# First sample by image halves in the opening, last sample stored in blocks, and constant matmuls in pauses of TensorE

## What is computed

```
x = x + _L0_conv_ref(_gn(x), ...)   # 3x3 conv, per-sample mixture of 3 experts, reflect pad
x = x + _L1_conv_ref(_gn(x), ...)   # |x|, depthwise 3x3
x = x + _L2_conv_ref(_gn(x), 8)     # 17x17 box mean
x = x + _L3_conv_ref(_gn(x), ...)   # sum of 8 neighbours, then 5 pointwise layers, 4 of them with elu

def _gn(v, G=8, eps=1e-05):         # mean and variance over 2 channels x 128 x 128
    g = v.reshape(B_, G, C_ // G, H_, W_)
    m = jnp.mean(g, axis=(2, 3, 4), keepdims=True)
    s = jnp.var(g, axis=(2, 3, 4), keepdims=True)
    return ((g - m) / jnp.sqrt(s + eps)).reshape(v.shape)
```

## Time and profile before

| | us |
|---|---|
| time, median of 3 runs (lowest, highest) | 721.12 (719.9, 723.21) |
| the profiled execution's own time | 722.67 |
| its span, first to last instruction | 720.9 |
| PE busy | 606.0 (84%) |
| DVE busy | 579.5 (80%) |
| ACT busy | 555.3 (77%) |
| POOL busy | 321.8 (45%) |

### The profile page before, as it was taken

One profiled execution on the slowest core, in us unless ns is written; L12 is line 12 of the kernel. 1 busy time (PEld: TensorE's weight loads), 2 busy tenths in 40 slices (PEclk: granted clock), 3 DMA queues, 4 the chain that ended last, 5 costly groups with the idle time before them and its releaser, 6 DMA issues.

```text
span 720.9 us, 13382 instructions
## 1 busy us (share of the span) xinstructions
PE 606.0 (84%) x4142; PEld 167.4 (23%) x4142; DVE 579.5 (80%) x1006; ACT 555.3 (77%) x1057; POOL 321.8 (45%) x487
## 2 busy tenths in 40 slices
PE   0355572899999999999999999999999899889981
PEld 0221220222222222222222222222222222222220
DVE  1453655688998899889988998898889788799992
ACT  0232100689999999999999999999999998988882
POOL 2530446136961797078717871777007800810000
PEclk9986676899999999999999999999999999999997
DMA  6769389629377728692868185718521820182002
GB/s 134 152 144 194 68 148 194 127 51 187 89 168 177 156 70 179 147 188 54 188 153 192 37 196 121 168 36 195 126 61 26 203 65 0 43 197 53 1 1 58
DMA packets 72890, 85.53 MB, mean 119 GB/s; under 512 B 8698, under 2 KB 58378, under 8 KB 72842
## 3 DMA queue, kind: packets, MB, share of 16 engines
q1 hardware_dynamic: 65488, 77.06, 49.4%
q10 hardware_dynamic: 7354, 7.87, 5.7%
HBM read 9.14 MB, written 8.39 MB: 24 GB/s over the span
## 4 chain that ended last, share of the span: by engine, by line
PE 45%; DVE 26%; ACT 12%; issue 8%; DMA 4%; SPq 1%; ACTq 1%; DVEq 1%; POOL 1%; POOLq 0%
PE pz L796 20%; PE pc L739 10%; DVE g L1001 8%; PE pc L773 7%; ACT u L659 5%; DVE bn L944 4%; ACT u L662 4%; DVE u L998 3%; DVE g_last L1001 3%; ACT u L665 3%; PE po L739 3%; PE po L805 2%; DMA win<-y 2%; DMA xs<-in_x_dram 2%; DVE xs L985 2%
## 5 line engine op out<-in xcount | busy, mean ns | idle before, releaser
L659 ACT ACTIVATE u<-pz 128x512 f32<-128x512 f32 x472 | 260.6, 601 | 67.4 <-PE pz L796 65.1
L796 PE MATMUL pz<-g,wT 64*64 64x512 f32 x1536 | 272.5, 610 | 18.6 <-DVE g L1001 16.7
L1001 DVE SCALAR_TENSOR_TENSOR g<-u,pz 128x512 f32<-128x512 f32 x384 | 247.9, 681 | 42.0 <-ACT u L662 37.7
L662 ACT ACTIVATE u<-u 128x512 f32<-128x512 f32 x472 | 275.7, 639 | 1.3
L796 PEld LDWEIGHTS pz<-g,wT 64*64 64x64 f32 x1536 | 69.2, 131 | 197.6 <-issue 196.1
L773 PE MATMUL pc<-win,t 64*32 64x512 f32 x1344 | 93.7, 630 | 8.2 <-DMA win<-y 5.8
L796 PE MATMUL pz<-stack,wT 64*64 64x512 f32 x512 | 86.7, 619 | 16.2 <-issue 10.3
L1001 DVE SCALAR_TENSOR_TENSOR g_last<-u,pz 128x512 f32<-128x512 f32 x128 | 82.7, 682 | 21.1 <-ACT u L662 19.3
L944 DVE BATCH_NORM_STATS2 bn<-xs 128x6 f32<-128x512 f32 (+1 forms) x128 | 84.6, 686 | 16.4 <-DMA xs<-in_x_dram 13.8
L739 PE MATMUL pc<-box_sum,box_mat 128*128 128x512 f32 x138 | 74.5, 634 | 1.3 <-DVE box_sum L1017 0.8
L459 POOL TENSOR_TENSOR stat<-stat 128x1 f32<-128x1 f32 x32 | 6.2, 195 | 132.8 <-DVE stat L959 132.8
(11 more groups left out here) (96 smaller groups left out, 504.2 us busy)
## 6 DMA issues: line engine op xcount, KB each, us to landing
stack<-near_sum SPq DMA_DIRECT2D x93, 192.0 KB, 3.9
win<-y SPq DMA_DIRECT2D x54, 260.0 KB, 4.4
win<-y SPq DMA_DIRECT2D x54, 195.0 KB, 4.5
out_dram<-xs SPq DMA_DIRECT2D x8, 1024.0 KB
stack<-box_sum SPq DMA_DIRECT2D x62, 128.0 KB, 3.8
xs<-in_x_dram SPq DMA_DIRECT2D x5, 1024.0 KB
stack<-near_sum SPq DMA_DIRECT2D x31, 128.0 KB, 2.9
win<-y ACTq DMA_DIRECT2D x10, 260.0 KB, 7.1
```

The costliest lines, as they stand in the source:

```text
L659: act.activation(u[:, m, :], pz[:, m, :], ACT.Relu, scale=-1.0, bias=0.0).then_inc(relu_done, 1)
L662: act.activation(u[:, m, :], u[:, m, :], ACT.Exp, scale=-1.0).then_inc(exp_done, 1)
L796: last = pe.matmul(pz[to, m, :], wT[rows, l, rows], src, start=True, stop=True)
L1001: dve.scalar_tensor_tensor(out=elus(l)[:, m, :], in0=u[:, m, :], scalar=-1.0, in1=pz[:, m, :], op0=ALU.add, op1=ALU.max).then_inc(g_writte ...
```

## The change

1. **Windows and convolutions of sample 0 (layers 0 and 1).** The windows are copied per quarter c: SP has c = 0 and 2, ACT c = 1 and 3. There are 26 DMAs for layer 0 (14 before) and 24 for layer 1 (12 before), for the same bytes. Each image half has a semaphore of its own, and `conv_taps` n writes chunks 2n and 2n + 1 and waits for the windows of its half alone. The other samples keep their windows.
2. **Constant matmuls.** `idle_turns(n)` issues n matmuls of 384 columns of the early constants into `po`, which nobody reads at that time. There are 4 behind a new wait for `setup_dve` >= 6, 3 ahead of layer 1 of sample 0, 4 and 5 ahead of and behind two `group_sums`, and 8 ahead of `rounds`: 24 in all.
3. **Last sample.** The store is 16 DMAs of 64 KB, one for each k, on SP except for the last two, which are on ACT. Each follows the `output` of its chunk.
4. **Clipping.** `clipped` no longer holds in the slot behind an `output`: slots 2, 11, 21 and 27 of the last sample and slot 27 of the one before, 5 halves in all, go back to two relus on ACT.

```diff
+        def clipped(j, q, l, a):
+            return (isinstance(j, int) and (j == B - 1 or j == B - 2 and q == Q - 1)
+                    and HALVES * q + 2 * l + a - 1 not in OUTPUT_AT)
...
+        def pair(i, k, n):
+            return (2 * n, 2 * n + 1) if isinstance(i, int) and i == 0 and k < 2 else (n, n + 2)
...
+        def windows_first(eng, k, c, last):
+            y, win, landed = ((y0, win0, win0_first), (y1, win1, win1_first))[k]
+            rows = around(y, win, c * KB, (c + 1) * KB, c % 2, last)
+            if k == 0 and not last and c % 3 == 0:
+                rows.append(edge0(c // 3))
+            for dst, src in rows:
+                eng.dma_start(dst, src).then_inc(landed[c // 2], 16)
...
+        def store_blocks(eng, j, first, end):
+            eng.wait_ge(out_evac, Q * j + (end - 1) // KB + 1)
+            for k in range(first, end):
+                eng.dma_start(ov[j][:, :, k, :], xs[:, j * N + k * W:j * N + (k + 1) * W]).then_inc(out_stored, 16)
...
-            windows0(sp, 0, (0,), True)
+            written(sp, 0, 0)
+            windows_first(sp, 0, 0, False)
+            windows_first(sp, 0, 0, True)
+            written(sp, 0, 1)
+            windows_first(sp, 0, 2, False)
+            windows_first(sp, 0, 2, True)
             load_blocks(sp, 2, 0)
...
-            store(B - 1)
-            sp.wait_ge(out_stored, B * LOAD)
+            for q in range(Q - 1):
+                store_blocks(sp, B - 1, q * KB, (q + 1) * KB)
+            store_blocks(sp, B - 1, K - KB, K - KB // 2)
+            sp.wait_ge(out_stored, (B - 1 + K) * LOAD)
...
+                    if isinstance(i, int) and i == 0:
+                        pe.wait_ge((win0_first, win1_first)[k][n], (FIRST0, FIRST1)[k])
+                    elif n == 0:
+                        pe.wait_ge((win0_in, win1_in)[k], (WIN0, WIN1)[k] * i)
...
-                                             blocks(win[m // 2], n + 2 * h)[rows, :, kw:kw + W], start=kw == 0, stop=kw == 2)
+                                             blocks(win[m // 2], pair(i, k, n)[h])[rows, :, kw:kw + W], start=kw == 0, stop=kw == 2)
...
+            def idle_turns(n):
+                table = con0[:, 0:3 * P]
+                for _ in range(n):
+                    pe.matmul(po[:, 0:3 * P], const("ones"), table, start=True, stop=True)
...
+            pe.wait_ge(setup_dve, 6)
+            idle_turns(4)
             group_sums(1, 0)
...
+            idle_turns(3)
             conv_taps(0, 1, 0, range(3))
             conv_taps(0, 1, 1, range(3))
+            idle_turns(4)
             group_sums(0, 2)
             group_sums(1, 1)
+            idle_turns(5)
...
             group_sums(1, 2)
+            idle_turns(8)
             rounds(pe, one)
```

More of the change, by code:

```diff
@@ L190, in build @@
         win1_in = sem("win1_in")
+        win0_first = [sem(f"win0_first{h}") for h in range(2)]
+        win1_first = [sem(f"win1_first{h}") for h in range(2)]
         stack_in = [sem(f"stack_in{h}") for h in range(2)]
@@ L234, in build @@
         SPREAD = 5
+        FIRST0 = 13 * 16
+        FIRST1 = 12 * 16
         WIN0 = 14 * 16
@@ L270, in pair_banks, with place @@
             return pc if at is None else pz[:, at:at + 2, :]
+        def pair(i, k, n):
+            return (2 * n, 2 * n + 1) if isinstance(i, int) and i == 0 and k < 2 else (n, n + 2)
+        def place(i, k, c):
+            return next((n, h) for n in range(2) for h in range(2) if pair(i, k, n)[h] == c)
         def chunk_bank(i, c):
@@ L316, in spread, with around @@
             eng.tensor_tensor(t0[:, :, :], t0[:, :, :], tpart[:, 1, :, :], ALU.add).then_inc(spread_step, 1)
-        def around(y, win, h, last):
-            a, b = h * WIN, WIN - h * WIN
-            lo, hi = h * K // 2, (h + 1) * K // 2
+        def around(y, win, lo, hi, swap, last):
+            a, b = swap * WIN, WIN - swap * WIN
             first, end = max(lo, 1), min(hi, K - 1)
@@ L334, in windows0 @@
                 eng.wait_ge(y0_written, Y0 * i + Y0 // 2 * (h + 1))
[L335 removed]
+                for dst, rows in around(y0, win0, h * K // 2, (h + 1) * K // 2, h, False) + [edge0(h)]:
                     eng.dma_start(dst, rows).then_inc(win0_in, 16)
[L337 to L339 removed]
             if last:
@@ L342, in windows0 @@
                 for h in range(2):
-                    for dst, rows in around(y0, win0, h, True):
+                    for dst, rows in around(y0, win0, h * K // 2, (h + 1) * K // 2, h, True):
                         eng.dma_start(dst, rows).then_inc(win0_in, 16)
@@ L349, in windows1 @@
                 eng.wait_ge(y1_written, Y1 * i + 2 * h + 2)
-                for dst, rows in around(y1, win1, h, False):
+                for dst, rows in around(y1, win1, h * K // 2, (h + 1) * K // 2, h, False):
                     eng.dma_start(dst, rows).then_inc(win1_in, 16)
@@ L354, in windows1, with written @@
                 for h in range(2):
-                    for dst, rows in around(y1, win1, h, True):
+                    for dst, rows in around(y1, win1, h * K // 2, (h + 1) * K // 2, h, True):
                         eng.dma_start(dst, rows).then_inc(win1_in, 16)
+        def windows_first(eng, k, c, last):
[5 more added lines that the diff above has]
+                eng.dma_start(dst, src).then_inc(landed[c // 2], 16)
+        def written(eng, k, h):
+            eng.wait_ge((y0_written, y1_written)[k], (Y0, Y1)[k] // 2 * (h + 1))
         def stacks(eng, i, h, banks):
@@ L630, in normal0 @@
                     act.wait_ge(norm_step[0], i * NORM + NORM)
-                    if not (isinstance(i, int) and i == 0):
-                        act.wait_ge(win0_in, WIN0 * i)
+                    if isinstance(i, int) and i == 1:
+                        for h in range(2):
+                            act.wait_ge(win0_first[h], FIRST0)
+                    elif not (isinstance(i, int) and i == 0):
+                        act.wait_ge(win0_in, WIN0 * (i - 1))
                 act.activation(blocks(y0, c)[:, :, 1:W + 1], sample(i, c).rearrange("p (k w) -> p k w", w=W), ACT.Identity,
@@ L643, in normal1 @@
                     act.wait_ge(norm_step[1], i * NORM + NORM)
-                    if not (isinstance(i, int) and i == 0):
-                        act.wait_ge(win1_in, WIN1 * i)
+                    if isinstance(i, int) and i == 1:
+                        for h in range(2):
+                            act.wait_ge(win1_first[h], FIRST1)
+                    elif not (isinstance(i, int) and i == 0):
+                        act.wait_ge(win1_in, WIN1 * (i - 1))
                 act.activation(blocks(y1, c)[:, :, 1:W + 1], sample(i, c).rearrange("p (k w) -> p k w", w=W), ACT.Abs,
@@ L1058, in one @@
                             full_stage(t + 2, at)
-                            if at in output_at and part_before(t, output_at[at]):
-                                output(*part_before(t, output_at[at]))
+                            if at in OUTPUT_AT and part_before(t, OUTPUT_AT[at]):
+                                output(*part_before(t, OUTPUT_AT[at]))
                             if has(t + 3):
```

73 lines of the change are left out of this document (43 added, 30 removed).

## The result

| | before | after |
|---|---|---|
| time, median (lowest to highest), us | 720.51 (719.89 to 723.21), 4 runs | 709.76 (709.53 to 711.49), 4 runs |
| the profiled execution: time / span, us | 722.67 / 720.9 | 709.53 / 707.4 |
| granted clock, mean over the span | 0.957 | 0.966 |

The ratio is 0.985, 95% interval 0.982 to 0.988: the change makes the kernel faster, by 10.75 us (1.5%) in the medians. The forecast was 702.4 from a median of 721.12, a gain of 18.7. The time lies 7.4 us above the forecast and 0.3 us above the range's upper end of 709.5.

What follows compares the result with a forecast made beforehand. TensorE, DVE and ACT were taken to pace the unchanged steady turns, late windows and half clock the opening. Opening 10.7 plus end 8.0 gave 18.7 us off 722.67, 704.0, less 1.55 for the median: 702.4 us; range 697.0 to 709.5.

Steps and rivals of the forecast that it cites:

- The store, 6.0: End of the kernel: only four 64 KB blocks remain after the last output, saving 6.0 us, from 5.0 to 7.1.
- Clipping, 2.0: Five slots behind an output: unclipped halves save 0.4 us each, 2.0 us together, from 0.5 to 2.9.
- First convolution at 32.1: Sample 0, layer 0: convolution 0 starts at 32.1 us, after matrix and sums, with the clock up or nearly so.
- Second convolution ends near 38.8: Sample 0, layer 0: convolution 1 waits for the second half at 35.9 and ends 5.6 us earlier than 44.4.
- the gain is held by the load until 42.1: Sample 2's load holds sample 1's windows, so its convolutions start 3.0 us earlier, not 5.6; bounds 1.5 and 5.6.
- Layer 1 of sample 0, 4.7 new: Layer 1 convolutions of sample 0 end at 70.3 instead of 78.04: 7.7 us gained, 3.0 kept and 4.7 new.
- The box, 2.8: Constants in the two pauses keep the clock up, so the first 12 box entries take 5.33 us, not 8.11.
- I keep 2.2 of it: Stack transfer behind the box: 2.2 us of the box's 2.8 survive sample 3's load; bounds 0 and 2.8.
- Before the turns, +0.8: Eight constant matmuls ahead of the turns raise the clock for the first entries: 0.8 us gained, bounds -1 and 1.5.
- the opening's 10.7: Total gain forecast before the steady turns: 7.7 + 2.2 + 0.8 = 10.7 us.
- transfers take more of the gain: Rival for the opening: smaller window DMAs move more slowly or contend more; gain 14.0 us, time 707.1, chance 0.20.
- The constants do not raise the clock: Rival: box keeps 8.11 us, turns start at half clock; gain 15.7 us, time 705.4, chance 0.06.

Runs made afterwards that it cites:

- after_again: The changed kernel (after), unchanged, run again beside later kernels on the same chip: 711.54 us, ratio 0.987 to the kernel before.
- end_only: The kernel before with only the 16-block last store and the five unclipped halves; opening as before: 711.36 us, ratio 0.987.
- load2_held: The changed kernel with SP's half of sample 2's load held until all layer 0 windows of sample 0 have landed: 712.72 us, ratio 0.990 to before.
- load3_early: The changed kernel with sample 3's load issued ahead of sample 1's layer 1 windows: 706.34 us, ratio 0.981 to before.
- wide_all: The changed kernel with the loads of samples 0 to 3 each as eight DMAs of 16 partitions: 703.47 us, ratio 0.978 to before.

## Why the prediction was wrong, step by step

- **The store, 6.0:** on the low side; it measured 7.1. The data of the last four blocks moves from 704.6 to 706.6, 2.0 us for the 2.1 of the sum. That of the single store moved until 720.2, thus for 9.2 us and not 8.4. The 64 KB blocks did not take the estimated 3.8 us that the Trainium skill's figure for a 64 KB load would give (0.95 us each; "DMA: Bandwidth & Descriptors", section "Bandwidth"): the whole stretch from issue to end is 4.0, lead and tail included.
- **Clipping, 2.0:** 2.7. A slot behind an output saved 0.54 and not 0.4. The last matmuls at half clock, -0.9, were not in the sum. The end: 8.9 for 8.0.
- **First convolution at 32.1:** right, at 30.83, or 31.86 on before's scale. It took 4.5 us in this profile where I had the clock up; in after_again and the other kernels with these windows and constants it took the 2.8 I had.
- **Second convolution ends near 38.8, and "the gain is held by the load until 42.1": the first step that failed.** I took the second half's landing from before, 35.9 or 34.9 shifted. It landed at 37.8, 2.9 late, and the convolution ran at half clock (4.42 us), 1.6 more. Of the 5.6 us at this place 1.1 was left before the question of who holds sample 1's windows arose: those were issued at 42.35, when the load had ended. They then took 15.0 us where before's took 14.3. The start of sample 1's convolutions gained 0.4 us (0.1 on end_only) and not 3.0, below my bound of 1.5. load2_held shows the cause, the load of sample 2: SP reaches it at 29.55, while ACT still issues windows, and it moves beside them. With SP's half of it held, all had landed by 33.5.
- **Layer 1 of sample 0, 4.7 new:** both convolutions at 2.8 us with no pause between, as forecast. The gain is 4.3 on before (0.4 to 4.7 in the table) and 1.2 on end_only, where the old code had the clock up too. That before's half clock here would recur was an assumption from one execution.
- **The box, 2.8:** right as a duration, 8.11 to 5.41; end_only had 7.35, which makes it 1.9.
- **"I keep 2.2 of it" behind the stack, and 0.8 before the turns: the second step that failed.** As a gain of the kernel both are near nothing: constants_only, which has all 24 constants on before, took 1.002 of its time (1.000 to 1.004), and after without them is not slower. Where the box's gain goes is less sure. On before it is lost at the stack with 0.5 more (16.5 us there, 19.7 in after); on end_only, with 19.7 as well, it is not. What is shown is the price of the load beside the stack, 12.9 to 13.5 us without and 16.5 to 20.9 with it. I saw that collision and treated it as a discount on the box's gain; it is a term of its own, larger than all that the constants could bring.
- **Before the turns, +0.8:** -0.8 on before. The last constant ended at 116.2, TensorE paused 5.3 us, and the first entries took 1.99 and 4.29 where before had 1.98 and 3.48. That was near my lower bound of -1. load3_early and wide_all, where the entry comes right behind the constants or 1.9 us later, show that the full clock is worth up to 2.4 us from there to the first output.

On before as it was profiled, 2.6, 0.4, 2.7 (the 2.2 and 0.5 more) and 1.6 are missing from the opening's 10.7, and 3.4 is left; on end_only 4.1 is left, and by the ratios 0 to 1.5. The store and the clipping, each too small in the sum, hid part of this: it is luck that the time missed the range by only 0.3 us. Of the rivals, "transfers take more of the gain" named the right mechanism, with 707.1 and a chance of 0.20; its sizes were too mild as well. "The constants do not raise the clock" was wrong in its reason and right in what it took off the sum: they raise it, and it was worth nothing. The range was too narrow since it let each case go wrong by itself, while at both landings the same thing, a load in flight, was at most a small discount in the sum.

## What to carry to other kernels

When an opening goes from transfer to transfer, write down for each landing what else is in flight, and count on little of a gain in compute ahead of it until that is gone. Prefetches belong in the stretch in which nobody waits for a transfer: in this kernel, moving one load forward by 16 to 21 us, cutting another differently and leaving out the last eight constants gave 12 to 14 us, more than the whole opening part of this change. Filler matmuls that keep the clock up were worth nothing while transfers were the chain, and a run of them ahead of a landing can itself become the wait. And take the base of such a sum from more than one execution: what before lost at half clock in layer 1, another kernel with the same opening did not.

## What the runs showed that I had not expected

- The load of sample 2 (1 MB from HBM) moves at about the same rate over twice as many busy engines (118 GB/s at a share of 0.61, 115 at 1.26), the load of sample 3 at 93 and 116 GB/s (0.62, 1.26). Copies within SBUF that share the engines with a load run at a joint 155 GB/s instead of 220 to 254.
- Small window DMAs are cheap to issue: 12 in 7.87 us, 0.66 us each, where I had feared 1.2. Twelve more, of layer 1, took 7.62 us at 53.39, where the DMA engines are full. Before, DMAs of twice the columns took 0.93 us each as the first of SP's queue (five in 4.64 us at 22.15) and 1.26 on ACT's. So the time of an issue went with its size here, and cutting the windows in two made each queue's issuing of sample 0's layer 0 longer by 0.8 us on SP (7.6 to 8.4) and 2.2 on ACT (6.2 to 8.4).
- The same opening can be 4.8 us apart at one place between two executions (stack issued at 110.30 and 105.48) and 1.5 us apart at the next landing (126.76 and 125.22): in the one with the early issue the load of sample 3 still moved for 8.8 us beside the stack, in the other for 6.2 at most.
